# A graph network's edge loop: VectorE's low half of the new state goes to the front of the odd turns

## The reference

```python
edge_attr = _swish(edge_attr_raw @ enc_W + enc_b)
for _ in range(STEPS):                                   # 4
    e_in = jnp.concatenate([edge_attr, x[src], x[dst]], axis=-1)
    e_upd = _layernorm(_swish(e_in @ eW1 + eb1) @ eW2 + eb2, eg, ebeta)
    edge_attr = edge_attr + e_upd
    agg = jax.ops.segment_sum(edge_attr, dst, num_segments=N_NODES)
    n_in = jnp.concatenate([x, agg], axis=-1)
    x = x + _layernorm(_swish(n_in @ nW1 + nb1) @ nW2 + nb2, ng, nbeta)
```

## Time and profile before

| | |
|---|---|
| median of 3 runs | 2535.23 us |
| profiled execution | 2531.88 us, span 2530.0 us |
| PE busy | 2363.9 us (93%) |
| PEld busy | 1852.1 us (73%) |
| DVE busy | 2224.7 us (88%) |
| ACT busy | 1914.2 us (76%) |
| POOL busy | 1627.2 us (64%) |
| `low_new` L1962 | 392 times, 686 ns |
| `scale` L1942 | 1568 times, 344 to 349 ns |
| `root` L310 to L324 | 9 per pair of groups, 161 to 228 ns |

### The profile page before, as it was taken

How to read it: one execution, slowest core, us unless ns; L and a number is a source line. 1 busy time by engine, 2 the same in 40 slices (tenths; PEclk the granted TensorE clock), 3 DMA queues, 4 the chain that set the end, 5 groups by cost and what they waited for, 6 DMA issues and landing times.

```text
span 2530.0 us, 82599 instructions
## 1 busy us (share of the span) xinstructions
PE 2363.9 (93%) x27988; PEld 1852.1 (73%) x27988; DVE 2224.7 (88%) x6127; ACT 1914.2 (76%) x5248; POOL 1627.2 (64%) x1588
## 2 busy tenths in 40 slices
PE   5799999999979999999988999999987999999995
PEld 2577777777747888888755787888864878788874
DVE  7699999999848999999965999999974899999996
ACT  3677777777548888888746888888854888888874
POOL 2777777777127777777406777777702777777750
PEclk9899999999999999999999999999999999999998
DMA  6666666776257888888536888888835676677740
GB/s 175 182 204 200 205 198 206 206 205 205 91 166 224 253 257 259 258 259 256 180 123 200 251 256 252 254 253 255 257 105 164 197 206 202 201 203 202 203 142 27
DMA packets 382921, 515.14 MB, mean 204 GB/s; under 512 B 58581, under 2 KB 256356, under 8 KB 382490
## 3 DMA queue, kind: packets, MB, share of 16 engines
q1 hardware_dynamic: 303572, 302.15, 37.1%
q0 software_dynamic: 75264, 205.62, 29.8%
q10 hardware_dynamic: 3654, 1.99, 0.3%
HBM read 390.48 MB, written 119.05 MB: 201 GB/s over the span
## 4 chain that ended last, share of the span: by engine, by line
PE 36%; POOL 31%; DVE 15%; issue 12%; DMA 4%; ACT 1%; DVEq 0%; ACTq 0%; SPq 0%; POOLq 0%
POOL arena L1646 31%; PE psum L1687 7%; PE psum L1714 6%; PE psum L1675 6%; DVE arena L1942 3%; DMA arena<-node_tables,idx_all 3%; PE psum L1745 3%; PE psum L2138 3%; PE psum L1667 3%; PE psum L2177 2%; DVE arena L1962 2%; PE psum L1699 2%; PE psum L2151 2%; DVE arena L1901 2%; PE psum L1709 1%
## 5 line engine op out<-in xcount | busy, mean ns | idle before, releaser
L1646 POOL DMA_INDIRECT arena<-node_tables,idx_all x1568 | 1613.7, 1029 | 809.9 <-issue 445.2
L1811 ACT ACTIVATE arena<-psum 128x1024 f16<-128x1024 f32 x392 | 401.5, 1024 | 401.0 <-PE psum L1687 401.0
L1901 DVE SCALAR_TENSOR_TENSOR arena<-psum,arena 128x1024 f16<-128x1024 f32 x392 | 478.7, 1221 | 151.4 <-PE psum L1714 79.5
L1714 PE MATMUL psum<-w_hi,arena 128*128 128x128 f16 x6272 | 589.3, 219 | 3.9 <-DVE arena L1901 3.9
L1714 PE MATMUL psum<-w_lo,arena 128*128 128x128 f16 x3136 | 545.5, 219 | 0.0
L1714 PEld LDWEIGHTS psum<-w_hi,arena 128*128 128x128 f16 x6272 | 498.3, 98 | 17.0 <-DVE arena L1901 5.2
L1687 PE MATMUL psum<-arena,w_hi 128*128 128x512 f16 x1568 | 469.6, 381 | 1.6 <-ACT arena L1848 1.6
L1675 PE MATMUL psum<-ident,arena 128*128 128x128 f16 x6272 | 418.0, 220 | 31.0 <-DMA arena<-node_tables,idx_all 30.4
L1675 PEld LDWEIGHTS psum<-ident,arena 128*128 128x128 f16 x6272 | 380.9, 98 | 55.2 <-DMA arena<-node_tables,idx_all 47.2
L1824 ACT ACTIVATE arena<-psum 128x128 f32<-128x128 f32 x1568 | 413.8, 290 | 5.5 <-PE psum L1714 5.5
L1812 ACT ACTIVATE psum<-psum 128x1024 f32<-128x1024 f32 x392 | 399.1, 1018 | 0.0
(11 more groups left out here) (177 smaller groups left out, 3080.9 us busy)
## 6 DMA issues: line engine op xcount, KB each, us to landing
state<-arena SPq DMA_DIRECT2D x294, 256.0 KB
arena<-state SPq DMA_DIRECT2D x294, 256.0 KB
arena<-node_tables SPq DMA_DIRECT2D x784, 64.0 KB
arena<-matrices SPq DMA_DIRECT2D x294, 128.0 KB
node_tables<-arena SPq DMA_DIRECT2D x100, 256.0 KB, 2.2
arena<-node_tables,idx_all POOLq DMA_INDIRECT x1568
arena<-rel_rows SPq DMA_DIRECT2D x98, 128.0 KB
matrices<-arena SPq DMA_DIRECT2D x98, 128.0 KB
```

The source lines that it names most:

```text
L1646: pool.indirect_dma_start(out=rows[n % R][:, t, :], out_offset=None, in_=p_table, in_offset=bass.IndirectOffsetOnAxis(ap=idx_all[:, n % G1 ...
L1714: x = pe.matmul(ps_v(k2)[:, t * P:(t + 1) * P], h[k2][:, half, t * P:(t + 1) * P], w[:, half, :], start=False, stop=half == 1 and h is hl, ...
L1811: act.activation(hh[k2], ps_h(k2), ACT.Silu).then_inc(S("hh"), 1)
L1901: dve.scalar_tensor_tensor(hl[k2], ps_h(k2), 1.0, hh[k2], ALU.mult, ALU.subtract).then_inc(S("hl"), 1)
```

## The change

In the odd turns `low_new` is called right behind `add_window`, ahead of the first root instruction. It stood between root instructions 7 and 8. Even turns stay as they were. The number of instructions is the same on every engine.

```diff
                     add_window(n - LAG - 3, w)
                     if n % 2:
+                        low_new(n - LAG - 2)
                         root(n - 3, 0, 2)
                         for t in range(TPG):
                             root(n - 3, t + 2, t + 3)
@@
                         root(n - 3, 6, 7)
                         add_old(n - LAG)
                         root(n - 3, 7, 8)
-                        low_new(n - LAG - 2)
                         root(n - 3, 8, 9)
                         gains(n - 1)
```

## The result

The kernel after takes 2569.64 us (median of 4 runs, 2561.18 to 2571.62), the kernel before 2533.68 us beside it (4 runs, 2530.49 to 2540.41). By the medians it is 36 us slower, where 15 us faster was forecast. The ratio on record is 1.0128, with a 95% interval of 1.0108 to 1.0148; the quotient of the two medians, 1.0142, lies inside it. The profiled execution took 2570.39 us, 38.5 us more than that of before.

What follows compares the result with a forecast made beforehand. It took VectorE to set the pace in step 0 and TensorE, waiting for the low half, in steps 1 to 3. +5.4 - 6.6 - 14.0 = -15.2 us gave 2520 us, range 2507 to 2541.

Steps and rivals of the forecast that it cites:

- -14.0 us: Steps 1 to 3: gain from TensorE's other 75 waits before L1745, 16.5 us less 2.5 returning as waits for gathered rows.
- TensorE's own 10.14: Steps 1 to 3: TensorE alone would need about 10.14 us a pair of turns, where it takes 10.37.
- Rival 1: Steps 1 to 3: GpSimd's gathers keep the pace, idle time before L1675 grows over 10 us; 2534 us, chance 0.21.
- Rival 2: All steps: VectorE becomes the bound, GpSimd holding L310 or L312 over 0.3 us in most turns; 2548 us, chance 0.14.
- +5.4 us: Step 0 cost: root instruction 8 waits for 7, 0.12 us in each of about 45 odd turns on VectorE.
- bound of 14.4: Step 0: upper bound of the cost, 0.12 plus 0.20 us for a hold on L310, over 45 odd turns.
- The wait before L1726 instead of L1741: Step 0: TensorE would wait 0.48 us for the scales before L1726, replacing 0.32 us before L1741, at no cost.
- -6.6 us: Ends of the steps: the three longest TensorE waits before L1745, 2.2 us each, are gained whole.

Runs made afterwards that it cites:

- three_after: Kernel after with three gathers a group instead of four (fourth tile's rows left out): 2497.24 us; the kernel before with the same edit took 2499.45 us.
- narrow_after: Kernel after with L1953 and L1962 narrowed to 8 of 512 columns in steps 1 to 3: 2507.45 us, ratio 0.9890.
- load_ahead: Kernel after with the next turn's window register load moved right behind issuing `low` in each odd turn: 2542.32 us, ratio 1.0029 to the kernel before.
- tail_only: Kernel before with the odd turns' low half one place forward, behind add_old and ahead of root instruction 7: 2573.84 us, ratio 1.0157.
- best2: Kernel before with odd turns reordered: step 0 root 6, low half, root 7, gains, root 8, window loaded early; steps 1-3 low half and add_old exchanged: 2524.63 us.
- front_gains: Kernel after with the gains (L1911) put between root instructions 7 and 8: 2546.43 us, ratio 1.0041 to the kernel before.

## Why the prediction was wrong, by its steps

- *"Part of that will come back as waits for gathered rows ... I allow for three more, 2.5 us, and take -14.0 us."* This step failed. The waits before L1745 went, as forecast, but 46.6 us of waits before L1675 came, and steps 1 to 3 grew by 27.3 us. The sum asked how fast TensorE could go and took GpSimd's gathers as 0.95 us each, whatever the order. Their length depends on what VectorE runs at the moment when they start, and it was the pace of these steps already: for step 2 the gathers give 8 x (0.989 + 0.305) = 10.35 us a pair before and 8 x (1.014 + 0.305) = 10.55 after, and the mean pairs from `low` to `low` are 10.38 and 10.57. TensorE's own 10.14 was right: the median pairs are 10.10 to 10.15 in three_after and 10.15 in narrow_after.
- *Rival 1, "GpSimd keeps the pace".* It named the right engine and was argued down with "the same engine follows at the shorter pair of step 1". It does, as long as few gathers are held. Its sign came: the idle time before L1675 grew by 46.6 us, where over 10 was asked. But it was priced at no gain, as if the gathers could not grow.
- *Rival 2.* It saw a hold between GpSimd and VectorE and looked at it from VectorE's side alone, L310 and L312. Its sign did not come: in steps 1 to 3 of the kernel after L310 is over 0.3 us in 1 of 141 odd turns, in the kernel before in 58. The hold that counts is the other way round, on GpSimd. The chance of 0.14 that it gave to a slower kernel went to another mechanism, and its 2548 us fell 22 short. The row to ask for was the mean of L1646 by step: 978 to 993 ns in the kernel before, where 945 is undisturbed.
- *"+5.4 us" for step 0.* The mechanism was right, the term too small: an odd turn grew by 0.29 us, not 0.12, and step 0 by 13.7. That lies inside the bound of 14.4, but not for its reason: 0.13 us is the dependence, close to the 0.12 of the forecast (load_ahead), and the rest is no hold on L310 but the sequencer's register load, a row that the busy times leave out. The wait before L1726 instead of L1741 came as written.
- *"-6.6 us" at the ends of the steps.* It fits what was measured outside the loops, -6.5 us; in tail_only, with the low half late, that remainder does not fall (+1.7).

How much of the stretch is bad luck can be estimated. A gather that starts x us into L1953 or L1962 loses 0.56 - x; added up over x from 0 to 0.56 that is 0.56 x 0.56 / 2 = 0.157. Four such instructions and eight gathers in a pair of 10.4 us give 8 x 4 x 0.157 / 10.4 = 0.48 us a pair, 24 us a step, if the starts were spread evenly (20 if the first 0.05 us are left out, in which L1953 holds none). What fell on gathers that started under these two is 22.7 us a step in the kernel after and 23.9 in tail_only, but 11.5 in the kernel before and 11.3 in best2; the scales add 2.6 to 4.0. So the old order stood in a favourable phase, at half of the even spread, and the change lost it. What fixes the phase, so that it could be chosen rather than found, stays open.

## What to carry to other kernels

Before pricing a move on one engine, plot the instruction length of its neighbours against it: where GpSimd's gathers run without a gap, each VectorE instruction with two SBUF inputs is a place at which they can stand still, and a move by a few tenths of a microsecond changes how many do. A wait that repeats every turn may be the effect of the engine that sets the pace, so count the work of that engine per step, start to end, before counting the wait as gain. And look at what an engine's sequencer does behind a dependent instruction: work that costs nothing under a queue shows up when the queue runs empty.

## What was not expected of the hardware

- A gather that starts inside a VectorE instruction with two SBUF inputs (128x512, 0.69 us) stands until that is 0.56 us old, not until its end; where the first input comes from PSUM, it is not held (in the traces of before, after, tail_only and front_gains 1087 gathers of steps 1 to 3 started under L1901 and 527 under L1911, and none took over 0.02 us more; of the 319 of step 0 none took over 0.12 us more). Under a scale of steps 1 to 3 (128x128, 0.35 us) it stands until that is some 0.23 us old.
- In the first 0.05 us of L1953 it is the other way round: the gather takes its usual time and L1953 0.07 us more.
- VectorE's register load of 0.30 us, with the 0.18 and 0.02 of the operations behind it, keeps the next instruction 0.73 us away; covered, it costs nothing, at the worst place 0.17 us a turn.
